# Masks off TensorE, score scaling on GpSimd, and new instruction orders in a fused attention kernel

## The reference

```
q, k, v = split(x @ Wqkv)            # 16 heads of 64
q = rotate(l2norm(q) * q_scale); k = rotate(l2norm(k) * k_scale)
sim = (q_window @ k_two_windows) * 8 # 32 queries see 64 keys
sim = where(mask, -max, sim)         # only the 33 keys up to the query's own
x = softmax(sim) @ v @ Wo + x
x = (a * gelu(gate)) @ W2 + b2 + x   # a, gate = split(layernorm(x) @ W1 + b1)
```

## Time and profile before

| | |
|---|---|
| median of 3 runs | 3868.3 us |
| the profiled execution | 3868.57 us |
| its span | 3866.5 us |
| mean granted TensorE clock | 0.978 |
| TensorE busy | 3499.5 us (91%) |
| VectorE busy | 2947.2 us (76%) |
| ScalarE busy | 1833.6 us (47%) |
| GpSimd busy | 1752.4 us (45%) |

### The profile page before, as it was taken

How to read it: one execution, slowest core, us unless ns; L and a number is a source line. 1 busy time by engine, 2 the same in 40 slices (tenths; PEclk the granted TensorE clock), 3 DMA queues, 4 the chain that set the end, 5 groups by cost and what they waited for, 6 DMA issues and landing times. The chain is left out here.

```text
span 3866.5 us, 75215 instructions
## 1 busy us (share of the span) xinstructions
PE 3499.5 (91%) x30204; PEld 1733.6 (45%) x30396; DVE 2947.2 (76%) x3288; ACT 1833.6 (47%) x2692; POOL 1752.4 (45%) x958
## 2 busy tenths in 40 slices
PE   6888857899999999999999999999999999999976
PEld 3222224454454545454454545454454545454543
DVE  6888747878787887878787878878787878878762
ACT  2677733444545454444545454444445454544432
POOL 2233024545454544545454545545454545445430
PEclk7999988999999999999999999999999999999998
DMA  6322133223233323333233323233332333232221
GB/s 201 79 50 51 26 109 68 61 65 68 69 70 72 78 55 69 71 76 72 61 66 69 75 68 76 60 68 72 75 75 60 68 69 73 68 75 60 64 46 44
DMA packets 178681, 271.11 MB, mean 70 GB/s; under 512 B 42913, under 2 KB 67489, under 8 KB 176673
## 3 DMA queue, kind: packets, MB, share of 16 engines
q1 hardware_dynamic: 174592, 251.85, 28.3%
q10 hardware_dynamic: 3744, 14.43, 1.0%
HBM read 45.25 MB, written 19.55 MB: 17 GB/s over the span
## 5 line engine op out<-in xcount | busy, mean ns | idle before, releaser
L1088 DVE SCALAR_TENSOR_TENSOR ly_prod<-ly_pj_ps,ly_gains,ly_tables 128x1024 f32<-128x1024 f32 x768 | 963.0, 1270 | 230.2 <-ACT ly_sq L1216 227.9
L919 PE MATMUL ly_pj_ps<-ly_xs,ly_wqk 128*128 128x512 f32 x1536 | 783.0, 616 | 102.6 <-DVE ly_prod L1088 80.3
L1216 ACT ACTIVATE ly_sq<-ly_pj_ps 128x512 f32<-128x512 f32 x768 | 450.6, 602 | 728.8 <-PE ly_pj_ps L919 464.0
L1000 PE MATMUL ly_to_ps<-ly_u,ly_mvo 128*128 128x512 f32 x1536 | 743.0, 602 | 0.9 <-DVE x_all L1159 0.9
L1318 POOL TENSOR_TENSOR ly_sx<-ly_sx,ly_smax 128x1024 f32<-128x1024 f32 x192 | 365.2, 1902 | 721.5 <-DVE ly_smax L1126 720.4
L1314 POOL TENSOR_TENSOR ly_qr<-ly_prod 128x1024 f32<-128x1024 f32 x192 | 454.4, 2367 | 324.7 <-DVE ly_prod L1088 323.5
L1314 POOL TENSOR_TENSOR ly_kr<-ly_prod 128x1024 f32<-128x1024 f32 x192 | 453.1, 2360 | 315.5 <-DMA ly_kbd<-ly_kr 290.1
L1247 ACT COPY ly_u<-ly_pair_ps 128x1024 f32<-128x1024 f32 x384 | 373.9, 1013 | 346.6 <-PE ly_pair_ps L988 346.6
L1323 POOL TENSOR_TENSOR ly_sx<-ly_sx,ly_rsum 128x1024 f32<-128x1024 f32 x192 | 365.3, 1903 | 264.5 <-DVE ly_rsum L1134 264.5
L919 PEld LDWEIGHTS ly_pj_ps<-ly_xs,ly_wqk 128*128 128x128 f32 x1536 | 266.9, 190 | 480.4 <-issue 275.5
L988 PE MATMUL ly_pair_ps<-ly_pt,ly_xt 32*128 32x512 f32 x3072 | 391.6, 623 | 48.2 <-DVE ly_hid L1152 26.1
(11 more groups left out here) (110 smaller groups left out, 3705.4 us busy)
## 6 DMA issues: line engine op xcount, KB each, us to landing
ly_qp<-ly_qr SPq DMA_DIRECT2D x768, 128.0 KB, 2.3
ly_kbd<-ly_kr SPq DMA_DIRECT2D x1536, 64.0 KB, 2.0
ga_parts_dram<-ga_parts SPq DMA_DIRECT2D x16, 384.0 KB, 2.3
ga_qs<-ga_parts_dram SPq DMA_DIRECT2D x96, 64.0 KB
ga_ks<-ga_parts_dram SPq DMA_DIRECT2D x96, 64.0 KB
ly_wqk<-in_wqk SPq DMA_DIRECT2D x24, 256.0 KB, 3.5
ly_mvo<-mvo_dram SPq DMA_DIRECT2D x6, 1024.0 KB, 5.2
mvo_dram<-ga_pt ACTq DMA_DIRECT2D x4, 1024.0 KB, 4.0
```

Source lines behind the costliest of these rows:

```text
L919: pe.matmul(pj_ps[:, j % 2, :], wqk[:, g, j % TILES, :], xs[:, n % 2, WIN:], start=True, stop=True).then_inc(proj_ready.sem, 1)
L1000: last = pe.matmul(to_ps[:], mvo[:, h, :], u[:, :, :, h, :].rearrange("p t c q -> p (t c) q"), start=(h == 0), stop=(h == LH - 1))
L1088: dve.scalar_tensor_tensor(prod[:, k], pj_ps[:, j % 2, :].unsqueeze(1).to_broadcast([P, 2, N]), gains[:, n // B, k:k + 1], tables[:, table ...
L1216: act.activation(sq[:, k, :], pj_ps[:, j % 2, :], ACT.Square).then_inc(sq_done.sem, 1)
```

## The change

- The mask is no longer written by TensorE. `mask_scores` (VectorE) reads the scores in PSUM and adds the mask, in the place of `scale_scores`. The mask is stored once per key and query, without the head axis, and the bf16 identity is gone.
- `scale_scores` is now a GpSimd step behind `less_max`: scores less their maximum, times one over the query norm.
- `rsqrt`: the first instruction and the squaring take the form of the others (scalar_tensor_tensor), with the constant of the first one in an SBUF column, broadcast.
- Five small constants are loaded as one array (`few`). The engines wait at the start for what they need and no longer for everything.
- `kbd_loaded` is two semaphores, by parity of the group. There is still one key buffer, and there are still six rotation tables.
- The bodies of all five engines are reordered.

The diff, cut. Of the bodies the new order is shown whole and the old one is left to the listing above.

```diff
-RSQRT_MAGIC = float(0x5F3759DF)
+MAGIC_BITS = float(np.array([0x5F3759DF], np.uint32).view(np.float32)[0])
...
-def rsqrt(eng, y, x, t, steps, batch, n):
-
-
-
-    eng.tensor_scalar(y.bitcast(I32), x.bitcast(I32), -0.5, RSQRT_MAGIC, ALU.mult, ALU.add).then_inc(steps.sem, 1)
+def rsqrt(eng, y, x, t, magic, steps, batch, n):
+
+    eng.scalar_tensor_tensor(y.bitcast(I32), x.bitcast(I32), -0.5, magic, ALU.mult, ALU.add).then_inc(steps.sem, 1)
     for i in range(3):
         eng.wait_ge(steps.sem, steps.at(batch, n + 3 * i + 1))
-        eng.tensor_tensor(t, y, y, ALU.mult).then_inc(steps.sem, 1)
+        eng.scalar_tensor_tensor(t, y, 1.0, y, ALU.mult, ALU.mult).then_inc(steps.sem, 1)
...
-        gains = sb("gains", [P, LAYERS, TILES])
-        b2 = sb("b2", [P, LAYERS])
+        few = sb("few", [P, NFEW])
+        gains = few[:, 0:LAYERS * TILES].rearrange("p (l j) -> p l j", j=TILES)
+        b2 = few[:, LAYERS * TILES:LAYERS * (TILES + 1)]
+        mean = few[:, NFEW - 2:NFEW - 1]
+        magic = few[:, NFEW - 1:NFEW].bitcast(I32)
 
...
-        mask = sb("mask", [P, 2, 512], BF16)
-        identb = sb("identb", [P, P], BF16)
+        mask = sb("mask", [P, T, SPAN], BF16)
...
-            sp.dma_start(gains[:], d["gains"]).then_inc(consts, 16)
-            for dst, src in ((tables, d["rot"]), (heads, d["heads"]), (ident, d["ident"])):
+            sp.dma_start(tables[:], d["rot"]).then_inc(early, 16)
+            sp.dma_start(few[:], d["few"]).then_inc(early, 16)
+            for dst, src in ((heads, d["heads"]), (ident, d["ident"])):
                 sp.dma_start(dst[:], src).then_inc(consts, 16)
             for g in range(1, UNITS):
                 load_wqk(0, g)
-            for dst, src in ((mask, d["mask"]), (identb, d["identb"]), (eps, d["eps"]), (centre, d["centre"]), (mean, d["mean"])):
+            for dst, src in ((mask, d["mask"]), (eps, d["eps"]), (centre, d["centre"])):
                 sp.dma_start(dst[:], src).then_inc(consts, 16)
-            sp.dma_start(b2[:], d["b2"]).then_inc(consts, 16)
             load_mvo(0)
             load_up(0)
-            sp.wait_ge(init, 2)
+            sp.wait_ge(kbd_set, 1)
 
...
+            # SyncE body
+                if x_1 is not None: keys(x_1, 0); next_wqk(x_1, 3)
                 if x_0 is not None: queries(x_0, 0)
+                if x_1 is not None: keys(x_1, 1)
+                if x_0 is not None: next_wqk(x_0, 0)
+                if x_1 is not None: keys(x_1, 2)
                 if x_0 is not None: queries(x_0, 1)
                 if x_1 is not None: keys(x_1, 3)
+                if x_4 is not None: next_up(x_4)
+                if x_0 is not None: queries(x_0, 2); next_wqk(x_0, 1); next_wqk(x_0, 2)
                 if x_2 is not None: next_mvo(x_2)
+                if x_0 is not None: queries(x_0, 3)
 
...
-            pe.wait_ge(init, 2)
-            pe.wait_ge(consts, 16 * 10)
...
+                elif g == 0:
+                    pe.wait_ge(consts, 16 * 5)
...
-                k = slot(("scores", n, g), s_scaled, s_scaled.at(n, g + 1))
-                for bank in range(2):
-                    pe.matmul(pair_ps[:, k, bank, :], identb[:], mask[:, bank, :], start=True, stop=False, skip_group_check=True)
+                k = slot(("scores", n, g), s_masked, s_masked.at(n, g + 1))
                 pe.wait_ge(qp_loaded.sem, qp_loaded.at(n, 16 * 4 * (g + 1)))
-                pe.wait_ge(kbd_loaded.sem, kbd_loaded.at(n, 16 * 8 * (g + 1)))
+                pe.wait_ge(kbd_loaded[g % 2].sem, kbd_loaded[g % 2].at(n, 16 * 8 * (g // 2 + 1)))
                 for t in range(T):
                     for p in range(2):
                         for c in range(4):
                             w, at = 4 * t + c, 256 * (t % 2) + 128 * p
                             last = pe.matmul(pair_ps[32 * c:32 * c + 32, k, t // 2, at:at + 128], qp[:, g, p, WIN * w:WIN * w + WIN],
-                                             kbd[:, p, :, WIN * w:WIN * w + SPAN], start=False, stop=True, skip_group_check=True)
+                                             kbd[:, p, :, WIN * w:WIN * w + SPAN], start=True, stop=True, skip_group_check=True)
                 last.then_inc(s_ready.sem, 1)
 
...
@@ -1031,40 +1034,40 @@
                 if x_4 is not None: spread_rstd(x_4)
                 if x_1 is not None: spread_norms(x_1, 0)
                 if x_4 is not None: up(x_4, 0)
+                if x_0 is not None: project(x_0, 3)
                 if x_2 is not None: attend(x_2, 2)
+                if x_0 is not None: project(x_0, 4)
                 if x_4 is not None: up(x_4, 1)
                 if x_1 is not None: scores(x_1, 0)
+                if x_0 is not None: square_sums(x_0, 0)
+                if x_1 is not None: spread_norms(x_1, 1)
                 if x_3 is not None: centred(x_3)
                 if x_0 is not None: project(x_0, 5)
                 if x_2 is not None: attend(x_2, 3)
+                if x_0 is not None: project(x_0, 6)
                 if x_4 is not None: up(x_4, 2)
+                if x_0 is not None: project(x_0, 7, 8)
+                if x_1 is not None: spread_norms(x_1, 2); scores(x_1, 1)
+                if x_0 is not None: square_sums(x_0, 1)
+                if x_1 is not None: spread_norms(x_1, 3)
                 if x_4 is not None: down(x_4)
+                if x_0 is not None: project(x_0, 9, 10)
+                if x_2 is not None: combine(x_2, 0, 1)
+                if x_1 is not None: scores(x_1, 2)
+                if x_2 is not None: combine(x_2, 2, 3, 4)
                 if x_1 is not None: token_transposes(x_1)
+                if x_0 is not None: project(x_0, 11)
+                if x_2 is not None: combine(x_2, 5)
+                if x_0 is not None: project(x_0, 12)
                 if x_2 is not None: combine(x_2, 6)
+                if x_0 is not None: square_sums(x_0, 2)
+                if x_1 is not None: scores(x_1, 3)
+                if x_0 is not None: project(x_0, 13, 14)
                 if x_2 is not None: combine(x_2, 7, 8, 9)
+                if x_0 is not None: project(x_0, 15)
+                if x_2 is not None: combine(x_2, 10, 11, 12)
                 if x_0 is not None: square_sums(x_0, 3)
+                if x_2 is not None: combine(x_2, 13, 14, 15)
                 if x_0 is not None: sums_by_token(x_0)
                 if x_3 is not None: variance(x_3)
                 if x_1 is not None: attend(x_1, 0)
...
-            dve.memset(kbd[:], 0.0).then_inc(init, 1)
-            dve.memset(xs[:], 0.0).then_inc(init, 1)
-            dve.wait_ge(init, 2)
-            dve.wait_ge(consts, 16 * 10)
+            dve.memset(xs[:], 0.0).then_inc(xs_set, 1)
+            dve.memset(kbd[:], 0.0).then_inc(kbd_set, 1)
+            dve.wait_ge(early, 32)
 
             def products(n, *tiles):
                 for j in tiles:
                     g, k = j // TILES, j % TILES
                     dve.wait_ge(sq_done.sem, sq_done.at(n, j + 1))
-                    if 8 * n + 2 * g >= 2 and k % 2 == 0:
-                        dve.wait_ge(rot_done.sem, 8 * n + 2 * g - 1 + k // 2)
+                    if UNITS * n + g and k % 2 == 0:
+                        dve.wait_ge(rot_done.sem, 2 * (UNITS * n + g - 1) + k // 2 + 1)
...
-                rsqrt(dve, rn[:, k % 2, lo:hi], ss[:, lo:hi], rt[:, lo:hi], steps, k, 1)
+                rsqrt(dve, rn[:, k % 2, lo:hi], ss[:, lo:hi], rt[:, lo:hi], magic.to_broadcast([P, hi - lo]), steps, k, 1)
...
             def scale_keys(n, g):
+                dve.wait_ge(rot_done.sem, rot_done.at(n, 2 * g + 2))
...
-            def scale_scores(n, g):
+            def mask_scores(n, g):
                 dve.wait_ge(s_ready.sem, s_ready.at(n, g + 1))
-                rq = rn[:, n % 2, 0:NSUM].rearrange("p (t r) -> p t r", t=T)[:, :, 4 * g:4 * g + 4]
                 if UNITS * n + g >= 2:
                     dve.wait_ge(pt_done.sem, UNITS * n + g - 1)
                 dve.tensor_tensor(sx[:, g % 2], pair_ps[:, where["scores", n, g]].rearrange("p b (t h k) -> p (b t) h k", h=4, k=SPAN),
-                                  rq.unsqueeze(3).to_broadcast([P, T, 4, SPAN]), ALU.mult).then_inc(s_scaled.sem, 1)
+                                  mask[:].unsqueeze(2).to_broadcast([P, T, 4, SPAN]), ALU.add).then_inc(s_masked.sem, 1)
 
...
+            # VectorE body
+                if x_1 is not None: mask_scores(x_1, 0); scale_keys(x_1, 1); score_maxima(x_1, 0)
+                if x_0 is not None: products(x_0, 4, 5, 6)
                 if x_4 is not None: gated(x_4, 2)
+                if x_1 is not None: scale_keys(x_1, 2)
+                if x_0 is not None: products(x_0, 7)
+                if x_1 is not None: mask_scores(x_1, 1); score_maxima(x_1, 1)
+                if x_0 is not None: products(x_0, 8)
                 if x_4 is not None: ffn_sum(x_4)
+                if x_1 is not None: prob_sums(x_1, 0)
                 if x_0 is not None: products(x_0, 9)
```

(67 more changed lines are left out.)

114 lines of the change are left out of this document (19 added, 95 removed).

## The result

The changed kernel takes 3762.78 us (median of 4 runs, 3754.45 to 3765.39), against 3867.2 (4 runs, 3862.63 to 3870.08). The ratio is 0.9727 (95% interval 0.9709 to 0.9746). That is 104 us less, where the prediction had 38 less: the side was right, and the size was too small by more than half. The time lies in the wide range of 3755 to 3880, which took in the rivals, but outside the forecast's own 3810 to 3850. It is close to what rival A named, but, as the trace shows, not by rival A's mechanism.

A forecast was written before the change was run, and what follows sets the result against it. It took TensorE's instruction stream, pinned to the VectorE chain at a few places, as the bound. From 3868.6 us, -36 for 48 bodies at -0.75, -6.5 at the start and +4 for GpSimd's extra pass gave 3830, range 3810 to 3850.

The forecast's parts named there:

- rival A: The norm chain is free of GpSimd's hold: product 0 ready 1.5 earlier, 2.25 per body, 3758 us; chance 0.15.
- the second stretch: TensorE from up 0 to up 1: stays 7.30 us after the square sums leave it, so 1.0 per body is lost.
- Masks: Mask matmuls removed from TensorE ahead of each scores block: 0.53 per block, taken as 2.0 us gained per body.
- Mask pass of VectorE: VectorE adds the mask in the pass that scaled the scores: 1.23 us as before, no change in cost.
- Norm chain: Chain before product 0: its new form is still held by GpSimd's rotations, so gain 0 and loss 0.1 per body.
- Key waits: TensorE's waits for key DMAs before scores 1, 2 and 3: the mean 0.3 stays as before.
- The third stretch: Up 1 to the down matmuls: projection 6 and up 2 each about 0.2 late, taken as 0.15 more per body.
- The score chain: Last scores block to attention: chain of 12.5 us equals TensorE's cover of 12.5, nothing to spare, cost taken as 0.
- Start and end: First projection at about 528, 6.5 us gained; the extra GpSimd pass uncovered in filling and draining, 4 us lost.
- B: The order removes more stalls: half the second stretch's 1.0 returns, the third loses nothing; 1.5 per body, 3794 us; chance 0.15.
- C: TensorE's freed time is all waited away at the same chain ends, only the start is won: 3866 us; chance 0.13.
- D: The score chain misses the last attention matmul by one GpSimd pass: +1.15 per body, 3921 us; chance 0.15.

The follow-up runs named there:

- e1: The changed kernel with one ScalarE pair swapped back, ffn_tokens(x_3) before gates(x_4, 0) as in the kernel before: 3808.14 us.
- e6: The changed kernel with the eight mask matmuls per body put back on TensorE, VectorE's mask pass staying too: 3846.4 us.
- e11: The changed kernel with scores 2 moved ahead of combines 0 and 1 on TensorE: 3818.14 us.
- e3: The changed kernel with GpSimd's last rotation of an item waiting until the norm chain is through: 3727.58 us.
- e5: The kernel before with only the norm chain's first instruction in the new form, its constant from a one-column tile: 3876.32 us.
- e7: The changed kernel with one more GpSimd pass, adding zeros, over group 3's scores between mask pass and scaling: 3875.33 us.
- e8: The changed kernel with TensorE and VectorE waiting at the start for all five constants of the layers: 3768.42 us.
- e12: The changed kernel with GpSimd's last rotation after the norm chain, product 1 directly behind product 0, and the first part's norm chain in the old form: 3705.5 us.
- e2: The kernel before without the eight mask matmuls of a body, the mask left out of the computation: 3839.64 us.

## Why the prediction was right or wrong

**The step that failed** is the second stretch: "so only 5.3 of work stands in the same 7.3: 1.0 is lost". The 7.30 was taken as fixed, since gelu, gated product and copies set both ends. It was fixed in the old ScalarE order only. The change also puts gates(x_4, 0) ahead of ffn_tokens(x_3); the line is in the diff, and I didn't follow it. With the swap the stretch is 6.38, and 0.1 is lost instead of 1.0. e1, which takes the swap back, has exactly the 7.29 of the prediction, and gives 0.86 of a body back: 41 of the 66 us that were missing.

**Per body, term by term.** Masks: -2.0 predicted, -1.77 measured (e6). Mask pass of VectorE: 0 predicted, 1.22 as before. Norm chain: +0.1 predicted; attention 0 to up 0 is 9.96 against 9.87, so +0.09. Second stretch: +1.0 predicted, +0.08 measured. Key waits: "the mean 0.3 of the key waits stays" was wrong, they fell to 0.03, so -0.28; that step looked at each DMA's end and not at the distance of the score blocks, and e11 shows that it is the distance that counts. These make -1.88 of the -2.15; each was taken from its own run or row, so that they add up is an assumption. The third stretch (+0.15 predicted) was not measured by itself. The rest, some -0.3, I read in the rows but didn't test: a score block and a block of square sums that touch follow each other 0.11 sooner (the row behind a score block starts 1.77 after it instead of 1.88), and the new order has three such places per body.

**What held.** The new links of the norm chain are held by GpSimd, whatever their form (the second link took the 2.33; e3, e5). The Trainium skill (SBUF — State Buffer, "SBUF: two separate sides") says that a VectorE operation with two SBUF inputs and a GpSimd operation that reads SBUF exclude each other, and that the one that starts first keeps the ports for its whole length; the trace agrees, with 2.33 against 0.30 for the same instruction. The score chain: the attention starts 12.65 behind scores 3, in the 12.5 to 12.8 given, and e7 shows that nothing was to spare.

**Start and end.** -6.5 + 4 predicted, about -3 in the spans. The sum is about right and its parts are not. The prediction had the first projection at 528, as if it waited for the tables; it waits for the first weights alone, 3.7 behind the layers' first DMA, 10.6 sooner than before. e8, which gives 8.0 of that back, costs 5.6 in time. And the new form in the first part, costed at nothing, moved the layers' first DMA by 8.8 to the other side (e12). So the first projection stands at 532.65. The 4 us for the extra GpSimd pass weren't measured by themselves.

**The rivals.** A gave 3758, within 5 us of the time, and is false (e5, and L61 in the changed kernel); that it came so near is chance. B asked for half of the 1.0 of the second stretch and gave 3794 (its own terms add up to 1.4 per body, not 1.5, and so to 3799); its direction was the true one, but it named the squares of ScalarE as the reason. C is what the masks do in the old order (e2), where 1.1 of the 1.77 that TensorE is freed of are not seen. D didn't happen, and would have cost some 2.4 per body (e7).

## What to carry to other kernels

When the orders of several engines change together, take each "fixed" interval apart by every engine that sets its ends, and look for moves on those engines in the diff; an interval is fixed only in the order in which it was measured. Work taken off the bounding engine is worth what the next wait allows: price it with the distance that a single buffer's refill needs (here 7.0 us), and look at the gap that a moved step enters as well as at the one it leaves. An experiment that undoes one line in each of the two kernels tells the worth of a line in both orders; here they differed by a factor of two to three. A helper that two parts share has to be priced in both.

## What the runs showed of the hardware

- ScalarE loads the table for gelu (1.28 us) as soon as it is free, beside the matmul whose result gelu waits for (the load from 2055.68, the matmul from 2055.84). With a copy in between, the same load is on the path, and the step comes 1.38 later (e1).
- A wait of 2.04 us of TensorE took the granted clock from 1.00 to 0.50 and made the attention and the projections behind it 1.6 us longer (e7), but only in 27 of 42 bodies; in the other 15 the same wait left it at 1.00. Between 740 and 3560 us the longest waits of TensorE in the changed kernel (1.55) and in e11 (1.91) left it at 1.00.
- A VectorE instruction of 0.30 us that starts beside a running GpSimd pass took 2.33 and ended with that pass (the changed kernel; 0.30 alone in e3).
